# L0 cross-attention: key norms and row maxima exchanged by DMA instead of by TensorE

## The reference

```
xn = layernorm(x, ln_x_g, ln_x_b)          # context, 1601 rows a batch
ln = layernorm(latents, ln_l_g, ln_l_b)    # latents, 64 rows a batch
q = (ln @ Wq).reshape(b, m, h, d).transpose(0, 2, 1, 3)      # 16 heads of 64
kv = jnp.concatenate([xn @ Wkv, ln @ Wkv], axis=1)
qn = rmsnorm(q, qn_g) * scale
kn = rmsnorm(k, kn_g)
sim = jnp.einsum('bhid,bhjd->bhij', qn, kn)
attn = jax.nn.softmax(where(mask, sim, max_neg))
out = jnp.einsum('bhij,bhjd->bhid', attn, v)
return out @ Wout + bout
```

## Time and profile before

| | us |
|---|---|
| three runs | 3403.0, 3399.54, 3392.83, median 3399.54 |
| profiled execution, its own time | 3395.09 |
| its span in the profile | 3392.6 |
| busy: TensorE, its weight loads, VectorE, ScalarE, GpSimd | 2876.9, 1943.1, 1615.2, 1080.2, 508.4 |
| mean granted clock of TensorE | 0.920 |

### The profile page before, as it was taken

One profiled execution on the slowest core, in us unless ns is written; L12 is line 12 of the kernel. 1 busy time (PEld: TensorE's weight loads), 2 busy tenths in 40 slices (PEclk: granted clock), 3 DMA queues, 4 the chain that ended last, 5 costly groups with the idle time before them and its releaser, 6 DMA issues. The chain is left out here.

```text
span 3392.6 us, 44228 instructions
## 1 busy us (share of the span) xinstructions
PE 2876.9 (85%) x17908; PEld 1943.1 (57%) x17908; DVE 1615.2 (48%) x3651; ACT 1080.2 (32%) x1931; POOL 508.4 (15%) x280
## 2 busy tenths in 40 slices
PE   4899999999999998579999968998964769588756
PEld 2465656666665665445565634665952449577644
DVE  4445454545545443425555545773531340355454
ACT  2233333333333331213555536641321423111121
POOL 2011020202011000000000002770010140244200
PEclk8899999999999999689999989998977879899877
DMA  3000000000000000030101000114857149423101
GB/s 132 0 1 22 1 22 22 1 22 1 22 1 22 1 1 4 27 134 21 40 20 40 1 6 23 45 35 176 312 192 252 55 149 311 166 87 108 31 1 31
DMA packets 80798, 215.22 MB, mean 63 GB/s; under 512 B 5328, under 2 KB 53992, under 8 KB 73944
## 3 DMA queue, kind: packets, MB, share of 16 engines
q1 hardware_dynamic: 77624, 204.32, 18.0%
q0 software_dynamic: 2976, 8.13, 0.7%
HBM read 201.33 MB, written 10.58 MB: 62 GB/s over the span
## 5 line engine op out<-in xcount | busy, mean ns | idle before, releaser
L1328 PE MATMUL L_xattn_bank<-L_xattn_keys_tok,L_xattn_probsT 119*128 119x257 f32 (+1 forms) x1792 | 437.6, 389 | 1.4 <-ACT L_xattn_probsT L1161 1.4
L1262 PE MATMUL L_xattn_wide<-L_xattn_keys_feat,weights_a 128*128 128x512 f32 (+2 forms) x1024 | 388.3, 524 | 3.0 <-DVE L_xattn_max L997 1.3
L1328 PEld LDWEIGHTS L_xattn_bank<-L_xattn_keys_tok,L_xattn_probsT 119*128 119x128 f32 (+1 forms) x1792 | 324.3, 189 | 112.3 <-ACT L_xattn_probsT L1161 42.6
L1155 ACT ACTIVATE L_xattn_scores<-L_xattn_scores,L_xattn_neg_max 128x833 f32<-128x833 f32 x128 | 119.7, 983 | 627.8 <-DVE L_xattn_neg_max L1002 627.8
L1262 PEld LDWEIGHTS L_xattn_wide<-L_xattn_keys_feat,weights_a 128*128 128x128 f32 x1024 | 190.6, 192 | 157.9 <-issue 128.8
L2267 DVE TENSOR_TENSOR_SCAN L_attn_state<-L_attn_decay,L_attn_banks 128x1024 f32<-128x1024 f32 x80 | 182.7, 2286 | 69.5 <-PE L_attn_banks L2469 61.5
L987 DVE TENSOR_TENSOR L_xattn_k_normed<-L_xattn_wide,L_xattn_k_normed 128x834 f32<-128x834 f32 x128 | 125.5, 1022 | 172.8 <-PE L_xattn_wide L1276 172.8
L1544 DVE CUSTOM_DVE_ANT_0 L_xattn_scores<-L_xattn_banks,L_xattn_mask 128x512 f32<-128x512 f32 (+1 forms) x256 | 131.5, 570 | 151.8 <-issue 151.8
L1082 POOL TENSOR_TENSOR L_xattn_keys_tok<-L_xattn_keys_tok,weights_a 119x1792 f32<-119x1792 f32 (+2 forms) x24 | 61.1, 2545 | 939.2 <-DVE L_xattn_keys_tok L922 939.2
L2373 POOL TENSOR_TENSOR L_attn_state<-L_attn_state,L_attn_C_rows 128x1024 f32<-128x1024 f32 x80 | 188.7, 2360 | 70.2 <-DVE L_attn_state L2267 70.1
L2469 PEld LDWEIGHTS L_attn_banks<-L_attn_B_diagonal,L_attn_dt_u_tok 128*128 128x128 f32 x1280 | 150.2, 193 | 66.3 <-issue 64.7
...
## 6 DMA issues: line engine op xcount, KB each, us to landing
...
```

The lines of the kernel that those rows point to most:

```text
L1262: last = nc.tensor.matmul(wide[:, 2 * h + c, 0:n], wk[:, k, p * P:(p + 1) * P], xnT[b % 2][:, k, a:a + n], start=(k == 0), stop=(k == KT - 1))
L1328: last = nc.tensor.matmul(bS[:, 0:D + 1], pT[0:r, c, a, :, :].rearrange("p h q -> p (h q)"), xn[b % 2][0:r, t, :], start=(t == 0), stop=(t ...
```

## The change

The spreading matmuls and the swap matmul are gone. In their place ScalarE issues DMAs: behind the Exp of `key_rnorm` eight (4 key groups x 2 heads), each of one row of `k_rnorm` (417 numbers) to 64 partitions of a new tile `k_scale`; and in a new `swap_max` two, each of 64 rows of `mx` (2 numbers) to the other 64 rows of a new tile. `keys_normed` reads `k_scale`; `shift` becomes a maximum and a multiplication by -1. ScalarE's `swap_max` and `exponentials` of step s, and VectorE's `keys_normed(s + 1)` and `shift(s)`, now stand at the end of turn s. On TensorE the parts of a turn are ordered anew, and mixing goes by `MIX_ORDER`, first the tiles whose weights ScalarE has turned. Since `spread` no longer writes all of `wide`, `scores` waits for the clamp that reads its first bank.

```diff
+    MIX_ORDER = [(c, a) for part in (range(4), range(4, HALF_T)) for c in range(2) for a in part]
+        spread = sb("k_scale", [P, 4, QK])
+        other = sb("max_of_other_half", [P, 2])
...
                 def keys_normed(s):
-                    dve.wait_ge(k_spread, s + 1)
+                    dve.wait_ge(k_scale_moved, 128 * (s + 1))
                     for x in range(2):
                         k = kn[:, s % 2, 2 * x * QK:2 * (x + 1) * QK].rearrange("p (a n) -> p a n", n=QK)
-                        nc.vector.tensor_tensor(k, wide[:, 2 * x:2 * x + 2, 0:QK], k, ALU.mult).then_inc(kn_ready, 1)
+                        nc.vector.tensor_tensor(k, spread[:, 2 * x:2 * x + 2, :], k, ALU.mult).then_inc(kn_ready, 1)
...
                 def shift(s):
-                    dve.wait_ge(swapped, s + 1)
-                    nc.vector.scalar_tensor_tensor(nm[:, :], mx[:, :], -1.0, bO[:, 320:322], ALU.mult, ALU.min
-                                                   ).then_inc(shifted, 1)
+                    dve.wait_ge(swapped, 32 * (s + 1))
+                    chain(nc.vector.tensor_tensor(mx[:, :], mx[:, :], other[:, :], ALU.max))
+                    nc.vector.tensor_scalar(nm[:, :], mx[:, :], -1.0, None, ALU.mult).then_inc(shifted, 1)
...
                     nc.scalar.activation(rk[:, :], rk[:, :], ACT.Exp, scale=-0.5).then_inc(k_rnorm, 1)
+                    act.wait_ge(k_rnorm, 2 * s + 2)
+                    if s >= 1:
+                        act.wait_ge(kn_ready, 2 * s)
+                    for j in range(4):
+                        for h in range(2):
+                            row = rk[32 * j + h:32 * j + h + 1, :].unsqueeze(1)
+                            nc.scalar.dma_start(spread[h * DH:(h + 1) * DH, j, :], row.broadcast_to([1, DH, QK])
+                                                ).then_inc(k_scale_moved, 16)
+
+                def swap_max(s):
+                    act.wait_ge(s_taken, 2 * s + 2)
+                    if s >= 1:
+                        act.wait_ge(shifted, s)
+                    for c in range(2):
+                        nc.scalar.dma_start(other[(1 - c) * S:(2 - c) * S, :], mx[c * S:(c + 1) * S, :]).then_inc(swapped, 16)
...
                 def scores(s):
                     b, p = divmod(s, NQ)
-                    pe.wait_ge(kn_ready, 2 * min(s + 1, STEPS - 1) + 2)
-                    if s + 1 == STEPS:
+                    pe.wait_ge(kn_ready, 2 * s + 2)
+                    if s + 1 < STEPS:
+                        pe.wait_ge(k_clamped, s + 2)
+                    else:
                         pe.wait_ge(s_taken, 2 * s)
...
                     if tiles[0] == 0:
                         pe.wait_ge(pT_even, 2 * s + 2)
-                        pe.wait_ge(pT_odd, 2 * s + 2)
                         if s >= 1:
                             pe.wait_ge(oh_ready, s)
-                    for t in tiles:
+                    if tiles[0] == 4:
+                        pe.wait_ge(pT_odd, 2 * s + 2)
+                    for i in tiles:
+                        c, a = MIX_ORDER[i]
+                        t = c * HALF_T + a
```

92 lines of the change are left out of this document (38 added, 54 removed).

## The result

| | before | after |
|---|---|---|
| runs | 3403.0, 3399.54, 3392.83, 3389.75 us | 5199.32, 5201.02, 5205.68, 5200.29 us |
| median | 3396.18 us | 5200.66 us |
| ratio | | 1.5316, 95% interval 1.5281 to 1.5351 |
| span of the profiled execution | 3392.6 us | 5197.4 us |
| mean granted clock of TensorE | 0.920 | 0.776 |

The change is slower, as forecast, and its time lies in the range. The likeliest case named 5415 us, 214 us too much. First the profile page of the changed kernel: the DMA's GB/s in the 40 slices, and the queues (packets, MB, share of 16 engines).

What follows compares the result with a forecast made beforehand. It took TensorE's work to bound the kernel's steps, with the score-to-turned-weights chain close. 3395.1 us + 1758 for the longer steps + 227 for the clock + 33 for the first step gave 5413, stated as 5415 us; range 3480 to 5650 us.

Steps and rivals of the forecast that it cites:

- likeliest case: Spreading DMAs limited by their source partition in SBUF, chance 0.55; 5415 us, spanning 5150 to 5600 us.
- A limit at the source: One SBUF source partition gives the spreading DMAs no more than one engine takes, 26.7 GB/s; chance 0.55.
- the signs named beforehand: Multiply waits some 30 us, last spread DMA lands about 34 us after issue, TensorE under half busy, clock falling, DMA near 17 GB/s.
- The bytes, 32.0 us: Time per step for the eight spreading DMAs to move 854 KB at 26.7 GB/s; other end 2.0 us.
- Issue 0.5 us each, fixed 2.4 us: ScalarE's queue is held 0.5 us per DMA, 4.0 us for eight; each landing has 2.4 us besides its bytes.
- rival of overlapping groups: DMAs from rows 0 to 33 and 64 to 97 overlap: bytes 16.0 us, 4389 us in total; chance 0.15.
- From T to the multiply: From the clamp's end, where scores start, to VectorE's multiply by the spread norms, when the last row lands: 35.6 us.
- From the multiply to the turned weights: VectorE's multiply 2.0 us, shift 0.4 us, then ScalarE's first exponential with its wait, 1.0 us.
- From there to T', 7.8 + 3.6 us for the clock: Turning, second half of keys, copy, square, means, clamp until next scores: 7.8 us; TensorE's lower clock adds 3.6 us.
- The first step, +33 us: The first step's norms are spread with nothing beside it, adding 33 us once.
- No limit at the source: DMA issue decides instead of the source partition: about 3490 us, from 3375 to 3620 us; chance 0.22.
- The faster case: Issue 0.32 us, landing 1.6 us, TensorE the bound, statistics steps losing their swap wait: saves 120 us, 3275 us; chance 0.08.

Runs made afterwards that it cites:

- run 1: The changed kernel with the same eight spreading DMAs, their order alternating between source rows 0 to 33 and 64 to 97; 4417.57 us.
- run 2: The changed kernel with each spreading DMA reading 64 partitions of squared keys instead of one norms row 64 times, key norms not applied; 3604.57 us.
- run 4: The changed kernel, DMA order kept, each DMA reading another copy of its norms row, so the sources lie in eight different groups of partitions; 4254.85 us.
- run 9: The kernel before, without the change's DMAs: VectorE's next-context statistics moved ahead of the multiply by norms, normalisation behind it; 3375.45 us, ratio 0.9928.

## Why the prediction was right, and by how much it was off

**What bounds the step.** Right. A limit at the source was given 0.55, and runs 1 and 2 single it out: same DMAs, another order or other sources, and the time falls by 783 and 1596 us. Of the signs named beforehand, the multiply's wait (29.46 us), TensorE's share (41%) and its clock (0.70) came.

**The bytes, 32.0 us.** 30.9. The rate was taken from one DMA engine at its best (26.7 GB/s) and the measured one is 27.7 GB/s, so 3% off. The reason given, one engine's worth from one partition, was not the mechanism: 13 to 14 of the 16 engines work, each packet taking 894 ns, and the limit belongs to a group of partitions (run 4). With the rows in their order both reasons give nearly the same time, so that the number came out does not speak for the forecast's reason; that part was luck. The last and first DMAs of the two groups overlap for some 4 us. The page of the Trainium skill named in the forecast ("SBUF — State Buffer", section on the port swizzle) gave an estimate of 31.4 us, by groups; the trace agrees within 0.6 us, for reads from SBUF.

**Issue 0.5 us each, fixed 2.4 us.** The issue's price was mis-sized as a fixed price: 22.4 us for the eight in the step shown, where 4.0 us were forecast, since from the fourth on they waited for slow DMAs (run 2: 0.62 us in the median). It cost nothing on the path here, as ScalarE had only the exponentials to do, which wait for the same DMA. In the turns where ScalarE also copies the next context's keys it held those up by 22.5 us, and the steps were no longer for it (one such step is 461.87 - 415.68 = 46.2 us). It also spoils one sign named beforehand: the landing of the last DMA is some 14 us behind its issue, not 34, since it is issued late. Read by that sign alone, the result would have looked nearer to the rival of overlapping groups (about 18 us). From T to the multiply the sum said 35.6 us, the trace says 495.16 - 461.87 = 33.3: bytes 1.1 less, first issue 0.3 earlier, fixed part 1.17 + 0.37 = 1.5 us instead of 2.4.

**From the multiply to the turned weights.** 498.48 - 495.16 = 3.3 us against 3.5 forecast (to T + 39.1).

**From there to T', 7.8 + 3.6 us for the clock.** 11.1 us against 11.4, but divided otherwise. The turning and the half of the keys take 504.48 - 498.48 = 6.0 us, against 0.76 + 2.88 = 3.6 us between starts before: the half of the keys by the earlier trace rows, the turning from 241.16 us there to the next row of the same timeline:

```profile
241.92 0.38 PE L1337 MATMUL L_xattn_bank<-const,L_xattn_mixed_tokens 128*128 128x128 f32 x2
```

So the clock costs 2.4 us and not 3.6, since it rises during the keys (0.50 up to 503.0 us). About 1 us more than forecast is mixing: the 8 matmul records at 505.77 (2.0 us) stand ahead of the means, where the forecast had the means at once behind the copy and the square. The mixing behind the scores was read too short as well: TensorE is idle from 470.36 us, T + 8.5 and not T + 6.7. That cost nothing, as it then waits for 28 us.

**The first step, +33 us.** +18.0. Before, the keys of the second step (8.90 us) and their norms came between the first norms and the first scores; now TensorE does those keys (90.50, 7.46 us) while the first DMAs run, and the second norms are spread inside the first step. The forecast had counted the landing in full and nothing beside it.

**The sum.** Per step 46.9 + 3.6 = 50.5 forecast, 47.7 in the step shown and 47.33 on average. 3.2 us x 63 = 200 us and 15 us of the start are the 214 us, to 1 us. In the step shown the 2.8 us too much are 2.3 up to the multiply, 0.2 up to the turned weights and 0.3 behind, where 1.2 us too much for the clock and 1 us too little for mixing nearly cancel.

**The rivals.** Overlap of the groups, 4389 us: run 1 has it at 4417.57, by a changed order. No limit at the source, about 3490 us and up to 3620: run 2 has 3604.57, with the bytes in 5.4 us and not in 2.0. The faster case had a landing of 1.6 us right for the maxima (1.6 to 1.8 us), and wrong that nothing comes between: a load in the same engines, and GpSimd at VectorE's second input. Its saving from the statistics was real but small: 24.8 us in run 9 of the 120 us that it was given together with the matmuls.

What stays open: how many DMAs of one queue run side by side, and why eight groups give 16.0 us and no less. Only one order of eight was run. How far a group reaches is shown only for the rows read here, and no run reads many partitions of one group at once.
